# Packed adjacency bytes turned by a DMA transpose of column pairs in a two-layer graph kernel

## The chip, the cores and the metric

The kernel runs on one core of a Trainium2 chip. The time is the device time of one execution in microseconds (us). A core has TensorE (PE; its weight loads are shown apart as PEld), VectorE (DVE), ScalarE (ACT), GpSimd (POOL) and SyncE (SP); 16 DMA engines move data, asked for by SP, ACT or POOL.

## The reference

x is 8192 x 128 in float32, adj is a symmetric 8192 x 8192 int32 matrix of zeros and ones with ones on the diagonal. Two layers follow one another:

```python
o1 = matmul((adj == 1), matmul(V, w1))        # adj == 2 and adj == 3 likewise with w2, w3: empty here
x = layernorm(x + o1 + o2 + o3 + bias)

h = x @ W.T + b
e = (h @ we1 + be1) + (h @ we2 + be2).T
e = where(e >= 0, e, 0.01 * e)
attention = softmax(where(adj > 0, e, -9e15), axis=1)
x = layernorm(x + attention @ h)
```

exp(leaky(e1 + e2)) splits into a product of a row factor and a column factor on either side of e1 + e2 = 0. So the second layer is, like the first, a product of 0/1 masks with tables: one mask of the edges with a positive sum, one of the others.

## The kernel before

The adjacency is read once, in 64 chunks of 1024 rows x 1024 columns: 8 row blocks S, and in each 8 column chunks c (k = 8 S + c). POOL loads a chunk in two halves into one of up to five buffers (L518; the DMA casts int32 to one byte), and asks for the load that reuses a buffer when the chunk that lay there is packed. DVE (`check_and_pack`, L571) packs eight rows of bytes into the eight bits of one byte, in a 128 x 1024 byte tile `pk` (L588). This tile has the rows of the matrix in the partitions, and the products need the columns there. So ACT converts it to bf16 with the byte order changed from (q j) to (j q) (`convert`, L999), TensorE transposes its eight 128x128 pieces into one PSUM bank (`turn`, L1192), and ACT writes the bank as bytes into the store of all edges, `E_raw` (`edges_of`, L1005). DVE then spreads the bits into fp8 masks (`spread`, L591): for layer 0 by `edge_masks` (L601) into `U0`, for layer 1 by `masks` (L606) into `UP`.

Layer 0 of a chunk is 32 TensorE products with 512 columns each (`layer0`, L1177; two halves of 16). After the eight chunks of a row block, its tail (y, the product with w1, layer norm, the score columns, the tables) runs over DVE, ACT, PE and SP; `tails(k)` gives its step by the slot. Layer 1 is 128 batches (`batch`, L1218), each one row half-block by one column chunk, and each 32 products: for every j of 8, two masks (positive in `UP`, negative in `gate_bufs`), and two tables. ACT makes a batch's gates with eight Sign activations of 128x512 into `gate_bufs` (`gates`, L1013); DVE ANDs them with the edges (L614) and XORs the rest (L616).

Each engine runs its own program in a fixed order over slots k = 0, 1, ... (loops at L823 for DVE, L1103 for ACT, L1277 for PE); semaphores alone tie them together. In slot k:

- DVE: `masks` of the slot's batches, `check_and_pack(k)`, `edge_masks(k-1, ...)`, pieces of the tails.
- ACT: `edges_of(k-1)`, gates of the batches of slot k+1, `convert(k)`, pieces of the tails.
- PE: `layer0(k-2, 0)`, `layer0(k-2, 1)`, the slot's batches, `turn(k)`, pieces of the tails.

48 of the 128 batches lie in slots up to 68, beside the chunks (`EARLY`); 80 follow when the whole adjacency has been read. At the end every finished half-block gets its product with W, its quotients, layer norm and a store.

Of the kernel before, what the change touches and what calls it, by code (L numbers as in the profile page):

```python
# [25 lines left out]
ACT = mybir.ActivationFunctionType  # L26
# [111 lines left out]
def build(nc, x, adj, w1, w2, w3, bias, W, b, we1, be1, we2, be2, out):  # L138
# [4 lines left out]
    with ExitStack() as ctx:  # L143
        def sb(name, shape, dt):
            return ctx.enter_context(nc.sbuf_tensor(name, shape, dt))
# [12 lines left out]
        tab_raw = sb("tables", [P, NS * 4 * JC * D], F16)  # L158
        in_raw = sb("adj_in", [P, 4 * 4 * CC], U8)
        seen = sb("seen", [P, 2 * CC], U16)  # L160
        pk = sb("packed", [P, CC], U8)
        pkb = sb("packed_bf16", [P, CC], BF16)
        U0 = sb("edge_masks", [P, 2 * JC * GR], U8)
        UP = sb("pos_masks", [P, 2 * JC * GR], U8)
        GN = sb("neg_masks", [P, 2 * JC * GR], U8)
# [72 lines left out]
        psT = ps[:, 2, :].bitcast(BF16)  # L238

        o_bank = ps[:, 3, :].rearrange("p (t c) -> p t c", t=GT)  # L240

        def o_of_bank(S, h):

            return ps[:, 2, :].rearrange("p (t c) -> p t c", t=GT) if h and S == NS - 1 else o_bank

        def z_bank(q, k):
            return ps[:, 4 + 2 * (q % 2) + k, :]
# [18 lines left out]
        def half(k, h):  # L266
            return homes[HOME[k]][:, 4096 * h:4096 * (h + 1)]

        def bits_of(S, c):
            n = (S * JB + c * JC) * P  # L270
            return E_raw[:, n:n + CC]


        def sems(*names):
# [7 lines left out]
        s_seen, s_p1, s_p2, s_pk, s_conv, s_turn, s_evac, s_u0, s_l0 = sems(  # L282
            "seen", "packed_4", "packed_2", "packed_1", "packed_converted", "packed_turned", "edges_ready",
            "edge_masks_ready", "layer0_multiplied")
# [274 lines left out]
        def _(e):  # L559
# [11 lines left out]
            def check_and_pack(k):  # L571
                e.wait_ge(s_adj[HOME[k]], 32 * FILL[k])
                a8, b8 = half(k, 0), half(k, 1)
                a, bb = a8.bitcast(U32), b8.bitcast(U32)
                w = CC // 4
                e.scalar_tensor_tensor(a, bb, 4, a, ALU.logical_shift_right, ALU.bitwise_or).then_inc(s_p1, 1)  # L576
                e.wait_ge(s_p1, k + 1)
                e.wait_ge(s_seen, k + 1)
                e.tensor_tensor(seen[:, :], seen[:, :], a8.bitcast(U16), ALU.bitwise_or).then_inc(s_seen, 1)  # L579
                e.wait_ge(s_seen, k + 2)  # L580
                low2 = a8[:, 0:2 * CC].bitcast(U16)
                e.tensor_scalar(low2, low2, 0x1111, None, ALU.bitwise_and).then_inc(s_half, 1)
                e.wait_ge(s_half, k + 1)
                e.scalar_tensor_tensor(a[:, 0:2 * w], a[:, 2 * w:], 0x22222222, a[:, 0:2 * w],
                                       ALU.bitwise_and, ALU.bitwise_or).then_inc(s_p2, 1)
                e.wait_ge(s_p2, k + 1)
                ge(e, s_conv, k)
                e.scalar_tensor_tensor(pk[:, :].bitcast(U32), a[:, w:2 * w], 2, a[:, 0:w],  # L588
                                       ALU.logical_shift_left, ALU.bitwise_or).then_inc(s_pk, 1)

            def spread(dst, src, h):  # L591

                src = src.bitcast(U16).rearrange("p (j i) -> p j i", j=JC)
                dst = dst.bitcast(U16).rearrange("p (j n i) -> p j n i", j=JC, n=GT)
                for n in range(GT):
                    by = 4 - BIT[4 * h + n]
                    shift = ALU.logical_shift_left if by >= 0 else ALU.logical_shift_right
                    ins = e.tensor_scalar(dst[:, :, n, :], src, abs(by), MASK, shift, ALU.bitwise_and)  # L598
                return ins

            def edge_masks(k, h):  # L601
                e.wait_ge(s_evac, k + 1)
                ge(e, s_l0, 2 * (k - 1) + h + 1)
                spread(U0[:, 4096 * h:4096 * (h + 1)], bits_of(k // NCH, k % NCH), h).then_inc(s_u0, 1)

# [382 lines left out]
        def _(e):  # L988
# [7 lines left out]
                e.wait_ge(s_vr, v + 1)  # L996
                e.activation(v_hl[:, 1, sl, :], x_in[:, sl, :], ACT.Copy, scale=LOW).then_inc(s_vl, 1)

            def convert(k):  # L999
                e.wait_ge(s_pk, k + 1)  # L1000
                ge(e, s_turn, k)
                e.activation(pkb[:, :].rearrange("p (j q) -> p j q", j=JC),  # L1002
                             pk[:, :].rearrange("p (q j) -> p j q", j=JC), ACT.Copy).then_inc(s_conv, 1)

            def edges_of(k):  # L1005
                e.wait_ge(s_turn, k + 1)
                if k >= 4 * NCH:
                    e.wait_ge(s_vl, NCH)
                if k >= (NS - 1) * NCH:
                    e.wait_ge(s_pk, GUEST[4] + 1)  # L1010
                e.activation(bits_of(k // NCH, k % NCH), psT, ACT.Copy).then_inc(s_evac, 1)  # L1011

            def gates(m):  # L1013
                q, g, c, _, _ = BATCH[m]
                if HELD[m] is not None:
                    e.wait_ge(s_bat, HELD[m] + 1)
                if GATE[m] == 2:
                    e.wait_ge(s_er, NS)
                e.wait_ge(s_row[q % 2], 16 * (q // 2 + 1))
                e.wait_ge(s_er, max(c, g // 2) + 1)  # L1020
                for j in range(JC):
                    n = GR * j
                    ins = e.activation(gate_bufs[GATE[m]][:, n:n + GR].bitcast(I8), e1row[:, q % 2, :], ACT.Sign,  # L1023
                                       bias=t2[:, JC * c + j:JC * c + j + 1])
                ins.then_inc(s_gate, 1)

# [76 lines left out]
            for k in range(NSLOT):  # L1103
                for S, off in tails(k):
                    if off == 3:
                        x1_of(S)
                if 1 <= k <= K:
                    edges_of(k - 1)
                if 1 <= k <= NCH:
                    split_low(k - 1)  # L1110
                for S, off in tails(k):
                    if off == 4:
                        e1_turned(S)
                        b_d_of(S)
                for m in at(k + 1):
                    if not fresh(m):
                        gates(m)
                for S, off in tails(k):
                    if off == 2:
                        sd_of(S)  # L1120
                    if off == 4 and not S:
                        high(S)
                if k < K:
                    convert(k)
# [51 lines left out]
        def _(e):  # L1176
            def layer0(k, h):  # L1177
# [4 lines left out]
                    e.wait_ge(s_y, 2 * (S - 1) + h + 1)  # L1182
                e.wait_ge(s_u0, 2 * k + h + 1)
                for j in range(JC):
                    n = 4096 * h + GR * j
                    for i, kind in enumerate((F8A, F8B)):
                        ins = e.matmul(ps[:, h, :], v_hl[:, i, JC * c + j, :], U0[:, n:n + GR].bitcast(kind),  # L1187
                                       start=c == 0 and j == 0 and i == 0,
                                       stop=c == NCH - 1 and j == JC - 1 and i == 1)
                ins.then_inc(s_l0, 1)  # L1190

            def turn(k):  # L1192
                e.wait_ge(s_conv, k + 1)
                ge(e, s_evac, k)
                for j in range(JC):
                    ins = e.transpose(psT[:, j * P:(j + 1) * P], pkb[:, j * P:(j + 1) * P], idb[:, :])  # L1196
                ins.then_inc(s_turn, 1)

            def o_of(S, h):
                e.wait_ge(s_y, 2 * S + h + 1)  # L1200
                if h:
                    if S < NS - 1:
                        e.wait_ge(s_v, 2 * S + 1)
                elif S:
                    e.wait_ge(s_e1Tc, S)
                else:
                    e.wait_ge(s_setc, 1)
# [10 lines left out]
            def batch(m):  # L1218
# [9 lines left out]
                e.wait_ge(s_pos, m + 1)  # L1228
                both = UP[:, 4096 * (m % 2):4096 * (m % 2 + 1)], gate_bufs[GATE[m]]
                for j in range(JC):  # L1230
                    n = GR * j
# [45 lines left out]
            for k in range(NSLOT):  # L1277
# [11 lines left out]
                if k < K:  # L1289
                    turn(k)  # L1290
                for m in at(k):
                    if first_of_all(m):
                        batch(m)
# [107 lines left out]
```

## Time and profile before

| | us |
|---|---|
| median of 3 runs | 1555.93 (1555.51 to 1557.21) |
| the profiled execution | 1557.76 |
| its span, from first to last instruction | 1556.1 |

| engine | busy us | share of the span |
|---|---|---|
| PE (products) | 1418.2 | 91% |
| PEld (weight loads, beside the products) | 669.7 | 43% |
| DVE | 1106.7 | 71% |
| ACT | 981.2 | 63% |
| POOL | 102.2 | 7% |

The profile page gives for each engine the time in which it was busy, then groups of instructions with their count, mean duration, and the idle time of the engine before them with what ended it. A row such as `PE ps L1196 <- ACT packed_bf L1002` says that TensorE sat idle before instructions of line 1196 until ACT had finished line 1002. The shares are means over the whole span; the kernel has three parts (a first one up to about 160 us, the rest of the chunks up to about 900 us, the batches alone after that), so the views below are also read stretch by stretch. The adjacency loads are in the page's queue 0 (software), everything that SP issues in queue 1 (hardware).

### The profile page before, as it was taken

Reading aid. Unit: us, or ns where it says so; the run is one execution under the profiler, and the core shown is the slowest. Engines: PE = TensorE matmul, PEld = TensorE weight load, DVE = VectorE, ACT = ScalarE, POOL = GpSimd, SP = SyncE. Lnnn points to the kernel's source line nnn. Section 1 sums busy time; section 2 is a strip of 40 time slices with the busy share of each in tenths; the row PEclk is TensorE's granted clock in tenths of the full one; section 3 lists DMA queues with packets and bytes.
Section 4 is the critical chain, followed back from the end, with each engine's and each line's share of the span. In section 5 each row is a group of like instructions: output and inputs, shape, how many; then the busy total and the mean of one; then the engine's idle time right before and its main releaser. Section 6 shows DMA issues by size and latency. Waiting matters only on the chain. (4 is left out here: it accounts for less than half of the span.)

```text
span 1556.1 us, 19556 instructions
## 1 busy us (share of the span) xinstructions
PE 1418.2 (91%) x6934; PEld 669.7 (43%) x6934; DVE 1106.7 (71%) x2561; ACT 981.2 (63%) x1584; POOL 102.2 (7%) x137
## 2 busy tenths in 40 slices
PE   0887798979999999999999997999999999999996
PEld 0434343444444444444444443444444444444443
DVE  2667777877977967967967946577667676666663
ACT  1334527446457457457457558678888788788873
POOL 2111111100110110100101000000000000000000
PEclk9989899999999999999999998999999999999998
DMA  9999999994979779886889421000110000100100
GB/s 125 145 126 116 130 107 140 115 108 76 83 100 115 83 74 102 114 83 75 113 85 102 82 95 55 8 1 28 48 34 28 28 28 27 55 27 28 35 1 15
DMA packets 88980, 114.32 MB, mean 73 GB/s; under 512 B 5104, under 2 KB 71216, under 8 KB 88880
## 3 DMA queue, kind: packets, MB, share of 16 engines
q0 software_dynamic: 67584, 67.12, 47.1%
q1 hardware_dynamic: 21296, 45.92, 8.6%
q8 instruction: 57, 0.93, 0.2%
q14 instruction: 43, 0.35, 0.1%
HBM read 298.06 MB, written 16.29 MB: 202 GB/s over the span
## 5 line engine op out<-in xcount | busy, mean ns | idle before, releaser
L1234 PE MATMUL ps<-pos_masks,tables 128*128 128x512 fp8e4 x2048 | 613.6, 381 | 39.6 <-DVE pos_masks L616 39.6
L1023 ACT ACTIVATE neg_masks<-e_row,cols 128x512 int8<-128x512 f32 x816 | 509.8, 709 | 109.0 <-PE ps L1234 58.4
L1234 PE MATMUL ps<-neg_masks,tables 128*128 128x512 fp8e4 x1632 | 489.7, 382 | 0.0
L1187 PE MATMUL ps<-edge_masks,tables 128*128 128x512 fp8e4 (+1 forms) x2048 | 463.9, 385 | 0.0
L1234 PEld LDWEIGHTS ps<-pos_masks,tables 128*128 128x128 f16 x2048 | 199.6, 98 | 285.8 <-issue 57.0
L1187 PEld LDWEIGHTS ps<-edge_masks,tables 128*128 128x128 f16 x2048 | 201.6, 99 | 233.2 <-issue 13.3
L1234 PEld LDWEIGHTS ps<-neg_masks,tables 128*128 128x128 f16 x1632 | 160.6, 98 | 195.8 <-issue 5.5
L614 DVE TENSOR_TENSOR neg_masks<-pos_masks,neg_masks 128x2048 uint16<-128x2048 uint16 x102 | 125.0, 1225 | 92.6 <-ACT neg_masks L1023 89.9
L598 DVE TENSOR_SCALAR pos_masks<-edges 128x512 uint16<-128x512 uint16 x512 | 114.4, 286 | 89.4 <-PE ps L1234 89.4
L1002 ACT ACTIVATE packed_bf<-packed 128x1024 bf16<-128x1024 uint8 x64 | 72.3, 1130 | 149.4 <-DVE packed L588 149.4
L598 DVE TENSOR_SCALAR edge_masks<-edges 128x512 uint16<-128x512 uint16 x512 | 124.2, 308 | 54.4 <-PE ps L1187 53.4
L1011 ACT ACTIVATE edges<-ps 128x1024 uint8<-128x1024 bf16 x64 | 65.1, 1017 | 148.1 <-PE ps L1196 147.8
L1023 ACT ACTIVATE y_turned<-e_row,cols 128x512 int8<-128x512 f32 x208 | 130.0, 707 | 22.5 <-DMA e_row<-e_scratch 12.1
L616 DVE TENSOR_TENSOR pos_masks<-pos_masks,neg_masks 128x2048 uint16<-128x2048 uint16 x102 | 124.9, 1225 | 3.5
L1234 PE MATMUL ps<-y_turned,tables 128*128 128x512 fp8e4 x416 | 123.7, 379 | 0.0
L1196 PE MATMUL ps<-idb,packed_bf 128*128 128x128 bf16 x512 | 42.5, 231 | 81.9 <-ACT packed_bf L1002 81.7
L518 POOL DMA_DIRECT2D adj_in<-adj x84 | 66.3, 793 | 536.4 <-DVE packed L588 525.0
L703 DVE TENSOR_TENSOR a_c_rows<-ps,a_c_rows 128x512 f32<-128x512 f32 x68 | 43.7, 684 | 52.1 <-PE ps L1234 48.9
L1196 PEld LDWEIGHTS ps<-idb,packed_bf 128*128 128x128 bf16 x512 | 35.0, 103 | 101.1 <-ACT packed_bf L1002 60.8
L576 DVE SCALAR_TENSOR_TENSOR adj_in<-adj_in 128x1024 uint32<-128x1024 uint32 x42 | 51.2, 1219 | 36.9 <-DMA adj_in<-adj 36.9
L1234 PEld LDWEIGHTS ps<-y_turned,tables 128*128 128x128 f16 x416 | 40.7, 98 | 49.1
L579 DVE TENSOR_TENSOR seen<-seen,adj_in 128x2048 uint16<-128x2048 uint16 x42 | 51.4, 1225 | 1.4
(134 smaller groups left out, 850.5 us busy)
## 6 DMA issues: line engine op xcount, KB each, us to landing
adj_in<-adj POOLq DMA_DIRECT2D x84, 512.0 KB, 13.7
tables<-adj POOLq DMA_DIRECT2D x28, 512.0 KB, 32.3
e_row<-e_scratch SPq DMA_DIRECT2D x34, 256.0 KB, 3.9
edges<-adj POOLq DMA_DIRECT2D x16, 512.0 KB, 12.5
part_scratch<-a_c_rows SPq DMA_DIRECT2D x18, 256.0 KB, 4.1
part_in<-part_scratch SPq DMA_DIRECT2D x18, 256.0 KB, 3.1
edges<-x SPq DMA_DIRECT2D x8, 512.0 KB, 6.6
x_rows<-x SPq DMA_DIRECT2D x8, 512.0 KB, 7.2
```

Source lines behind the costliest of these rows:

```text
L518: e.dma_start(half(k, h).bitcast(F8C).rearrange("p (b c) -> p b c", b=GT), block_rows(adj, S)[:, GT * h:GT * (h + 1), c * CC:(c + 1) * CC])\
L576: e.scalar_tensor_tensor(a, bb, 4, a, ALU.logical_shift_right, ALU.bitwise_or).then_inc(s_p1, 1)
L579: e.tensor_tensor(seen[:, :], seen[:, :], a8.bitcast(U16), ALU.bitwise_or).then_inc(s_seen, 1)
L598: ins = e.tensor_scalar(dst[:, :, n, :], src, abs(by), MASK, shift, ALU.bitwise_and)
L614: e.tensor_tensor(n, u, n, ALU.bitwise_and).then_inc(s_neg, 1)
L616: e.tensor_tensor(u, u, n, ALU.bitwise_xor).then_inc(s_pos, 1)
L1002: e.activation(pkb[:, :].rearrange("p (j q) -> p j q", j=JC), pk[:, :].rearrange("p (q j) -> p j q", j=JC), ACT.Copy).then_inc(s_conv, 1)
L1011: e.activation(bits_of(k // NCH, k % NCH), psT, ACT.Copy).then_inc(s_evac, 1)
L1023: ins = e.activation(gate_bufs[GATE[m]][:, n:n + GR].bitcast(I8), e1row[:, q % 2, :], ACT.Sign, bias=t2[:, JC * c + j:JC * c + j + 1])
L1187: ins = e.matmul(ps[:, h, :], v_hl[:, i, JC * c + j, :], U0[:, n:n + GR].bitcast(kind), start=c == 0 and j == 0 and i == 0, stop=c == NCH ...
L1196: ins = e.transpose(psT[:, j * P:(j + 1) * P], pkb[:, j * P:(j + 1) * P], idb[:, :])
L1234: ins = e.matmul(z_bank(q, k), tab[:, c, 2 * k + i, j, :], mask[:, n:n + GR].bitcast(F8A), start=first and j == 0 and i == 0, stop=final a ...
```

## The change

The eight TensorE transposes of a chunk, the conversion in front of them and the PSUM evacuation behind them go. In their place ACT issues one DMA transpose for each chunk, in the slot and at the place where it converted. It works on 2-byte elements, so a pair of neighbouring bytes moves together; therefore the last packing step writes `pk` in a new order, with the pair index outermost, through 16-bit instead of 32-bit words; it reads its two sources with a step of 8 bytes. In the partition of one column pair the bytes of columns 2j' and 2j'+1 now alternate. The masks and the gates keep that order: `place(mask, j)` names the 512 bytes of one j, which lie every second byte, and both the ACT instruction that writes a gate and the TensorE products that read a mask use it. `pk` has two buffers, each with a semaphore of its own; the packing waits for the transpose of two chunks ago. Products of the first layer's second half with w1 get a PSUM bank of their own in all row blocks (bank 2, free now), and with it one wait goes.

```diff
-        pk = sb("packed", [P, CC], U8)
-        pkb = sb("packed_bf16", [P, CC], BF16)
+        pk = sb("packed", [P, 2, CC], U8)
...
         def o_of_bank(S, h):
-            return ps[:, 2, :].rearrange("p (t c) -> p t c", t=GT) if h and S == NS - 1 else o_bank
+            return ps[:, 3 - h, :].rearrange("p (t c) -> p t c", t=GT)
...
+        def place(mask, j):
+            return mask[:, 2 * GR * (j // 2):2 * GR * (j // 2 + 1)].rearrange("p (i two) -> p two i", two=2)[:, j % 2, :]
...
             # check_and_pack, DVE
-                ge(e, s_conv, k)
-                e.scalar_tensor_tensor(pk[:, :].bitcast(U32), a[:, w:2 * w], 2, a[:, 0:w],
+                if k >= 2:
+                    e.wait_ge(s_edges[k % 2], 16 * (k // 2))
+                w1, w0 = [a8[:, CC * n:CC * (n + 1)].bitcast(U16).rearrange("p (q j) -> p j q", j=JC // 2)
+                          for n in (1, 0)]
+                e.scalar_tensor_tensor(pk[:, k % 2, :].bitcast(U16).rearrange("p (j q) -> p j q", j=JC // 2), w1, 2, w0,
                                        ALU.logical_shift_left, ALU.bitwise_or).then_inc(s_pk, 1)
...
             # spread, DVE
-                src = src.bitcast(U16).rearrange("p (j i) -> p j i", j=JC)
-                dst = dst.bitcast(U16).rearrange("p (j n i) -> p j n i", j=JC, n=GT)
+                src = src.bitcast(U16).rearrange("p (j i) -> p j i", j=JC // 2)
+                dst = dst.bitcast(U16).rearrange("p (j n i) -> p j n i", j=JC // 2, n=GT)
...
             # edge_masks, DVE
-                e.wait_ge(s_evac, k + 1)
+                e.wait_ge(s_edges[k % 2], 16 * (k // 2 + 1))
...
             # ACT, in slot k where convert(k) stood; edges_of(k - 1) at the slot's start is gone
-            def convert(k):
+            def turn(k):
                 e.wait_ge(s_pk, k + 1)
-                ge(e, s_turn, k)
-                e.activation(pkb[:, :].rearrange("p (j q) -> p j q", j=JC),
-                             pk[:, :].rearrange("p (q j) -> p j q", j=JC), ACT.Copy).then_inc(s_conv, 1)
...
-                e.activation(bits_of(k // NCH, k % NCH), psT, ACT.Copy).then_inc(s_evac, 1)
+                e.dma_start_transpose(bits_of(k // NCH, k % NCH).bitcast(U16).rearrange("p (j q) -> p j q", j=JC // 2),
+                                      pk[:, k % 2, :].bitcast(U16)).then_inc(s_edges[k % 2], 16)
...
             # gates, ACT
-                    ins = e.activation(gate_bufs[GATE[m]][:, n:n + GR].bitcast(I8), e1row[:, q % 2, :], ACT.Sign,
+                    ins = e.activation(place(gate_bufs[GATE[m]], j).bitcast(I8), e1row[:, q % 2, :], ACT.Sign,
...
             # layer0, PE
-                        ins = e.matmul(ps[:, h, :], v_hl[:, i, JC * c + j, :], U0[:, n:n + GR].bitcast(kind),
+                        ins = e.matmul(ps[:, h, :], v_hl[:, i, JC * c + j, :],
+                                       place(U0[:, 4096 * h:4096 * (h + 1)], j).bitcast(kind),
...
             # PE
-            def turn(k):
-                e.wait_ge(s_conv, k + 1)
-                ge(e, s_evac, k)
-                for j in range(JC):
-                    ins = e.transpose(psT[:, j * P:(j + 1) * P], pkb[:, j * P:(j + 1) * P], idb[:, :])
-                ins.then_inc(s_turn, 1)
...
             # o_of, PE
-                if h:
-                    if S < NS - 1:
-                        e.wait_ge(s_v, 2 * S + 1)
-                elif S:
+                if S:
                     e.wait_ge(s_e1Tc, S)
...
             # batch, PE
-                            ins = e.matmul(z_bank(q, k), tab[:, c, 2 * k + i, j, :], mask[:, n:n + GR].bitcast(F8A),
+                            ins = e.matmul(z_bank(q, k), tab[:, c, 2 * k + i, j, :], place(mask, j).bitcast(F8A),
```

## Rows read from the trace of the kernel before

**Rows 1.** Busy time by stretch: start:end, length, then each engine's busy us (instructions), clock, DMA.

```profile
core 0: us, PE busy (x) PEld busy (x) DVE busy (x) ACT busy (x) POOL busy (x), PEclk, DMA share, GB/s
0.00:160.00 160.00, 99.11 (x473) 48.57 (x474) 96.06 (x210) 54.32 (x72) 27.74 (x42) 0.93 1.09 127
160.00:280.00 120.00, 102.39 (x517) 48.31 (x514) 92.43 (x223) 60.65 (x100) 14.20 (x19) 0.94 1.12 125
280.00:400.00 120.00, 106.54 (x529) 50.79 (x529) 94.40 (x211) 62.10 (x102) 10.97 (x14) 0.96 0.81 97
...
637.00:754.00 117.00, 116.10 (x594) 55.55 (x593) 93.38 (x211) 69.90 (x117) 11.00 (x14) 1.00 0.77 91
...
1000.00:1250.00 250.00, 249.19 (x1182) 116.81 (x1181) 171.92 (x414) 204.13 (x325) 0.51 (x1) 1.00 0.08 26
```

**Rows 2.** Waits in 0 to 160 us: waiting line, releaser, total us, times, longest us.

```profile
PE ps L1196 <- ACT packed_bf L1002: 58.7, 9, 29.7
...
DVE adj_in L576 <- DMA adj_in<-adj: 34.7, 6, 20.6
...
DVE tables L576 <- DMA tables<-adj: 15.7, 6, 5.1
```

**Rows 3.** Timeline of DVE, first stage, the last packing step of four chunks (start, duration).

```profile
61.50 0.42 DVE L588 SCALAR_TENSOR_TENSOR packed<-tables 128x256 uint32<-128x256 uint32 x1
...
72.73 0.42 DVE L588 SCALAR_TENSOR_TENSOR packed<-adj_in 128x256 uint32<-128x256 uint32 x1
```

**Rows 4.** The same, after the last piece of x has been loaded.

```profile
126.24 0.42 DVE L588 SCALAR_TENSOR_TENSOR packed<-adj_in 128x256 uint32<-128x256 uint32 x1
...
136.14 0.42 DVE L588 SCALAR_TENSOR_TENSOR packed<-tables 128x256 uint32<-128x256 uint32 x1
```

**Rows 5.** Waits over the whole span.

```profile
PE ps L1196 <- ACT packed_bf L1002: 81.7, 17, 29.7
...
DVE edge_masks L598 <- ACT edges L1011: 0.8, 1, 0.8
```

**Rows 6.** Waits of TensorE and DVE in 520 to 900 us.

```profile
PE ps L1234 <- DVE pos_masks L616: 4.6, 4, 1.9
...
DVE adj_in L576 <- DMA adj_in<-adj: 2.2, 1, 2.2
```

**Rows 7.** Timeline at 748 us: the transposes' weight loads, then layer 0's, on TensorE.

```profile
748.39 0.65 PEld L1196 LDWEIGHTS ps<-idb,packed_bf 128*128 128x128 bf16 x8
...
749.00 6.63 PEld L1187 LDWEIGHTS ps<-edge_masks,tables 128*128 128x128 f16 x32
```

**Rows 8.** Chain that ended last: start, us, what; 256 products in a row.

```profile
1445.05 55.25 PE ps L1234 x256
```

**Rows 9.** Groups by line and form: busy us, mean ns of one, idle before.

```profile
L1023 ACT ACTIVATE neg_masks<-e_row,cols 128x512 int8<-128x512 f32 x816 | 509.8, 709 | 109.0 <-PE ps L1234 58.4 <-issue 39.8 <-DMA e_row<-e_scratch 10.8
...
L1002 ACT ACTIVATE packed_bf<-packed 128x1024 bf16<-128x1024 uint8 x64 | 72.3, 1130 | 149.4 <-DVE packed L588 149.4
...
L1011 ACT ACTIVATE edges<-ps 128x1024 uint8<-128x1024 bf16 x64 | 65.1, 1017 | 148.1 <-PE ps L1196 147.8
...
L584 DVE SCALAR_TENSOR_TENSOR adj_in<-adj_in 128x512 uint32<-128x512 uint32 x42 | 29.1, 693 | 1.4
...
L588 DVE SCALAR_TENSOR_TENSOR packed<-adj_in 128x256 uint32<-128x256 uint32 x42 | 17.8, 424 | 1.4
```

**Rows 10.** Timeline at 760 us on DVE: a chunk packed, and its masks begun.

```profile
760.48 0.42 DVE L588 SCALAR_TENSOR_TENSOR packed<-adj_in 128x256 uint32<-128x256 uint32 x1
...
770.18 0.89 DVE L598 TENSOR_SCALAR edge_masks<-edges 128x512 uint16<-128x512 uint16 x4
```

**Rows 11.** DMA issues: KB each, median us from issue to landing.

```profile
part_in<-part_scratch SPq DMA_DIRECT2D x18, 256.0 KB, 3.1
...
x_rows<-x SPq DMA_DIRECT2D x8, 512.0 KB, 7.2
```

**Rows 12.** DMA queue of SP: packets, MB, share of 16 engines over the span.

```profile
q1 hardware_dynamic: 21296, 45.92, 8.6%
```

More of the change, by code:

```diff
@@ L237, in build @@
         ps = ctx.enter_context(nc.psum_tensor("ps", [P, 8, GR], F32))
-        psT = ps[:, 2, :].bitcast(BF16)
-        o_bank = ps[:, 3, :].rearrange("p (t c) -> p t c", t=GT)
         def o_of_bank(S, h):
-            return ps[:, 2, :].rearrange("p (t c) -> p t c", t=GT) if h and S == NS - 1 else o_bank
+            return ps[:, 3 - h, :].rearrange("p (t c) -> p t c", t=GT)
         def z_bank(q, k):
@@ L281, in build @@
         s_adj = [sem(f"adj_in_{n}") for n in range(5)]
-        s_seen, s_p1, s_p2, s_pk, s_conv, s_turn, s_evac, s_u0, s_l0 = sems(
-            "seen", "packed_4", "packed_2", "packed_1", "packed_converted", "packed_turned", "edges_ready",
-            "edge_masks_ready", "layer0_multiplied")
+        s_seen, s_p1, s_p2, s_pk, s_u0, s_l0 = sems(
+            "seen", "packed_4", "packed_2", "packed_1", "edge_masks_ready", "layer0_multiplied")
+        s_edges = [sem(f"edges_ready_{n}") for n in range(2)]
         s_y, s_xg, s_xb, s_o, s_v, s_st, s_mv, s_var, s_sd, s_rs, s_nm, s_x1 = sems(
@@ L997, in split_low @@
                 e.activation(v_hl[:, 1, sl, :], x_in[:, sl, :], ACT.Copy, scale=LOW).then_inc(s_vl, 1)
-            def convert(k):
+            def turn(k):
                 e.wait_ge(s_pk, k + 1)
-                ge(e, s_turn, k)
-                e.activation(pkb[:, :].rearrange("p (j q) -> p j q", j=JC),
-                             pk[:, :].rearrange("p (q j) -> p j q", j=JC), ACT.Copy).then_inc(s_conv, 1)
-            def edges_of(k):
-                e.wait_ge(s_turn, k + 1)
                 if k >= 4 * NCH:
                     e.wait_ge(s_vl, NCH)
-                if k >= (NS - 1) * NCH:
-                    e.wait_ge(s_pk, GUEST[4] + 1)
-                e.activation(bits_of(k // NCH, k % NCH), psT, ACT.Copy).then_inc(s_evac, 1)
+                e.dma_start_transpose(bits_of(k // NCH, k % NCH).bitcast(U16).rearrange("p (j q) -> p j q", j=JC // 2),
+                                      pk[:, k % 2, :].bitcast(U16)).then_inc(s_edges[k % 2], 16)
             def gates(m):
@@ L1021, in gates @@
                 for j in range(JC):
-                    n = GR * j
-                    ins = e.activation(gate_bufs[GATE[m]][:, n:n + GR].bitcast(I8), e1row[:, q % 2, :], ACT.Sign,
+                    ins = e.activation(place(gate_bufs[GATE[m]], j).bitcast(I8), e1row[:, q % 2, :], ACT.Sign,
                                        bias=t2[:, JC * c + j:JC * c + j + 1])
@@ L1106, in _ @@
                         x1_of(S)
-                if 1 <= k <= K:
-                    edges_of(k - 1)
                 if 1 <= k <= NCH:
@@ L1123, in _ @@
                 if k < K:
-                    convert(k)
+                    turn(k)
                 if k < NCH:
@@ L1184, in layer0 @@
                 for j in range(JC):
-                    n = 4096 * h + GR * j
                     for i, kind in enumerate((F8A, F8B)):
-                        ins = e.matmul(ps[:, h, :], v_hl[:, i, JC * c + j, :], U0[:, n:n + GR].bitcast(kind),
+                        ins = e.matmul(ps[:, h, :], v_hl[:, i, JC * c + j, :],
+                                       place(U0[:, 4096 * h:4096 * (h + 1)], j).bitcast(kind),
                                        start=c == 0 and j == 0 and i == 0,
@@ L1230, in batch @@
                 for j in range(JC):
-                    n = GR * j
                     for k, mask in enumerate(both):
                         for i in range(2):
-                            ins = e.matmul(z_bank(q, k), tab[:, c, 2 * k + i, j, :], mask[:, n:n + GR].bitcast(F8A),
+                            ins = e.matmul(z_bank(q, k), tab[:, c, 2 * k + i, j, :], place(mask, j).bitcast(F8A),
                                            start=first and j == 0 and i == 0, stop=final and j == JC - 1 and i == 1)
@@ L1288, in _ @@
                         after(m)
-                if k < K:
-                    turn(k)
                 for m in at(k):
```

## The prediction

> **What bounds the kernel now.** I read the busy time by stretch first, since the shares over the whole span mix three parts [rows 1]. From 1000 us on TensorE is busy 249.19 of 250 us: batches alone, and no chunk is turned there. From 637 to 754 us, which is eight chunks (14.63 us each), it is busy 116.10 of 117 us; DVE has 93.38 and ACT 69.90. So between about 400 and 900 us TensorE sets the pace, and what it no longer has to do is time won. The waits agree: from 520 to 900 us the batches waited for DVE for only 4.6 us, and DVE for a load of adjacency for 2.2 us [rows 6]. The first 160 us are different. TensorE is busy 99.11 of 160 us, the DMA share is 1.09 [rows 1], and DVE waited 34.7 + 15.7 us for adjacency, 20.6 of it for the first chunk [rows 2]. Chunks are packed every 11.23 us (61.50 to 72.73) while a 512 KB piece of x comes with each, and every 9.90 us (126.24 to 136.14) afterwards [rows 3, 4]. This is the pace of the loads: some 12 chunks are DMA-bound. From 160 to 400 us, some 17 chunks, TensorE is busy 87% (102.39 + 106.54 of 240), the loads still fill the DMA engines in the first half (1.12) but DVE hardly waits for them, and TensorE loses the rest to waits and to stretches at the lower clock (mean granted 0.94 and 0.96) [rows 1].
>
> **TensorE loses the transposes.** The weight loads of eight transposes begin at 748.39 and those of the next products at 749.00, so turning a chunk holds TensorE for 0.61 us [rows 7]. (The durations of single matmuls overlap; I count starts.) In the 12 DMA-bound chunks that is worth nothing, since TensorE idles there anyway. In the other 52 it is 52 x 0.61 = 31.7 us. That holds for the 35 chunks from 400 us on without doubt, and for the 17 before them as far as TensorE is on the path; it is at 87%, so I count them too.
>
> **TensorE loses a wait.** It waited 81.7 us for the converted bytes [rows 5], 58.7 of them in the first 160 us, where 29.7 is the start [rows 2]. Behind 160 us there are 81.7 - 58.7 = 23.0 us. In their place TensorE goes on to layer 0 two chunks back, whose masks come from DVE; next late are DVE's masks and the tails. So of the 23 us I take a third, 8 us, with 0 and 20 as ends. The bank for the second w1 product takes a wait on DVE away at seven places; it was short of the path, and I count nothing.
>
> **ACT.** It loses a conversion of 1130 ns and an evacuation of 1017 ns for each chunk [rows 9], 2.15 us, and the waits for TensorE in front of the evacuation. It gets the issue of a DMA. Its hold on ACT's queue is in no row; gates, high parts of tables and exponentials are queued behind it. ACT idles 117 - 69.90 = 47 us in eight chunks, 5.9 us each [rows 1], so with the 2.15 us freed a hold of up to 8 us a chunk fits on average. Cost 0 for the likely case; above 8 us ACT would be the bound.
>
> **The gates and the strided masks.** ACT now writes every second byte. The nearest rows are the two operations of 1024 elements: with bytes read at a step of 8 it took 1130 ns, with dense ones 1017 [rows 9]. Scaled to 512 elements that is 57 ns on 709, at most 0.46 us for the eight gates of a batch. In the last part ACT is busy 204.13 of 250 us [rows 1], so it goes to 87% and stays hidden by TensorE except at the ends of half-blocks; I take 0, with up to +8 us. The 6144 products of 512 columns read fp8 at a step of 2 bytes. They start 55.25 / 256 = 0.216 us apart [rows 8], one column per tick of the 2.4 GHz clock, which a dense row of bytes doesn't show to be free at a step of two. I take 0 and keep the other case as a rival.
>
> **DVE.** The last packing step goes from 256 words (424 ns) to 512 half-words; the row with 512 elements took 693 ns [rows 9]. That is +0.27 us a chunk, 17 us in all, with DVE at 80% in the steady part [rows 1]: hidden. A step of 8 bytes may add to it; even a doubling is hidden. The masks are spread with as many elements as before. The new wait in front of the packing is on a transpose of two chunks ago, which is old by then.
>
> **Latency of the transpose.** `edge_masks` waits for it. Queued behind that wait on DVE are the masks of the next batches and the next packing. A chunk packed at 760.90 has its masks begun at 770.18, and it is among the tightest [rows 10]; in the DMA-bound part it is about 9.5 us as well. Today DVE waits 0.8 us for the evacuation in all [rows 5]. Transfers of SP landed in 3.1 us (256 KB) and, beside the loads, 7.2 us (512 KB) [rows 11]. A chunk is 128 KB, so 3 to 7 us are hidden. Beyond 9 us DVE would stall, and TensorE behind it.
>
> **DMA work of the transpose.** This is the cost that matters, because it adds to each chunk in the DMA-bound part: x us more of the 16 engines give 12 x. Lower bound: 512 KB of x stretched a chunk by 11.23 - 9.90 = 1.33 us, so 128 KB cost 0.33 us [rows 3, 4]. Upper bound: SP's queue shows 21296 packets in 8.6% of 16 x 1556.1 us, 0.10 us a packet [rows 12]; if a chunk is cut into 512 pieces of 256 bytes it costs 512 x 0.10 / 16 = 3.2 us. I take 1.0 us, between them in ratio: +12 us, ends +4 and +38. From 160 us on it is covered: the loads need 9.90 us of the 14.63 us of a chunk.
>
> The two rules of the Trainium skill that bear on this contradict each other. "DMA: Bandwidth & Descriptors", in its list of oddities, gives the DMA transpose 261 GB/s; by an estimate from it 128 KB take 0.5 us, the term would be +6 us and the forecast 1526. "VectorE: DVE Perf Modes", section on the three transpose paths, puts a 128x128 transpose at 1309 ns by DMA and 390 ns on TensorE, and advises TensorE where PSUM will do as the destination, which speaks against this change. On the TensorE side the trace disagrees if it is meant as a rate: eight took 0.61 us, 76 ns each [rows 7]. If its DMA figure were work of the engines, an estimate gives four blocks 5.2 us a chunk, the rival B below.
>
> **Clock.** In the first 160 us the mean granted clock is 0.93 with TensorE 62% busy [rows 1]. It will do slightly less and idle in one piece instead of two. Half a dozen more short stretches at 1.2 GHz could cost a few us where TensorE is just late: +4, between 0 and +12.
>
> **Sum.** -31.7 - 8 + 12 + 4 = -24 us on the span of 1556.1. The profiled execution (1557.76) lies 1.8 us above the median of 1555.93; on the median it gives 1532. With the ends of the terms: -31.7 - 20 + 4 = -48, 1508; -21 (if the 17 middle chunks give nothing) - 0 + 38 + 12 + 8 = +37, 1593.
>
> **Rival A: more than the sum.** The coupling of ACT and TensorE in both directions goes, and the middle part gets the whole of its waits back: 1495 to 1510. For it: ACT waited for TensorE in front of L1011 for 147.8 us [rows 9]. Against: most of that is idle time which ACT has anyway. Chance 0.13.
>
> **Rival B, the slower side: the DMA engines.** The transposes compete with the adjacency loads. In the first 12 chunks each us counts; beyond 14.63 - 0.61 - 9.90 = 4.1 us all other 52 chunks become DMA-bound too. The change is lost from x = 3.0 on (12 x 3 = 36 = 31.7 + 8 - 4). At x = 4.5: 54 + 52 x 0.4 = 75, less 36, is +39: 1595. At x = 5.2: 62 + 57 - 36 = +83: 1639. For it: a DMA share of 1.09 and 1.12 up to 280 us [rows 1], and a transpose may move small pieces. Against: 128 KB are little beside the 1 MB of bytes that a chunk's load writes. A hold of over 8 us on ACT would look much the same in time. Chance 0.26.
>
> **Rival C: strided operands.** If TensorE reads bytes at a step of two at half rate, 6144 x 0.216 = 1327 us are added: 2860. A loss of 2% would already eat the gain. Nothing in the trace speaks for it but that no row shows the step. Chance 0.05.
>
> **Rival D: nothing.** The gain in the middle part and the loss in the first cancel (x near 3, or half the gain): 1553 to 1559. Chance 0.06. The forecast, 1510 to 1553, has 0.50.
>
> **How the numbers follow.** 0.2%, 3 us, is about what a measurement of this kernel can tell from no change. Faster: 0.50 + 0.13 = 0.63; same 0.06; slower 0.26 + 0.05 = 0.31. The range leaves out C, the part of B beyond 1600 (some 0.08), and half of A: 1500 to 1600.
>
> **What the profile will show.** The 0.61 us: eight chunks in the steady part take 117.0 - 4.9 = 112 us. The first part: the spacing of packings is 9.90 + x. ACT: no wait before the place where it converted, and gates near 709 ns. Latency: DVE's wait before `edge_masks` stays near nothing. Strides: TensorE's products still start 0.216 us apart, and the packing step takes some 0.69 us. I am wrong if the spacing in the first part is over 13 us, if DVE waits for the transposes, or if ACT's activations stand apart by many us after each issue.

## The result, and the profile after

| | before | changed |
|---|---|---|
| median of 4 runs, us | 1556.33 (1555.51 to 1557.21) | 1600.79 (1600.12 to 1601.61) |
| span of the profiled execution, us | 1556.1 | 1599.7 |

The ratio is 1.0287, with a 95% interval of 1.0275 to 1.0299: 44 us slower. The forecast was 1532 us, faster, with a range up to 1600.

The busy time by stretch, in the columns of [rows 1]:

```profile
core 0: us, PE busy (x) PEld busy (x) DVE busy (x) ACT busy (x) POOL busy (x), PEclk, DMA share, GB/s
0.00:160.00 160.00, 84.95 (x346) 36.38 (x346) 88.55 (x188) 23.95 (x29) 26.37 (x40) 0.91 1.10 130
160.00:280.00 120.00, 91.15 (x400) 40.56 (x401) 87.33 (x202) 34.60 (x79) 13.70 (x18) 0.87 1.12 126
...
637.00:754.00 117.00, 110.96 (x513) 50.47 (x510) 91.27 (x199) 52.50 (x96) 11.03 (x14) 0.99 0.84 100
...
1000.00:1250.00 250.00, 242.00 (x1138) 112.87 (x1137) 169.22 (x391) 203.36 (x325) 0.51 (x1) 0.99 0.10 29
```

TensorE lost work and did not become faster for it: in the steady part it is busy 110.96 of 117 us where it was 116.10. ACT lost what it should, 52.50 us against 69.90. The last chunk is packed at 931.0 us against 886.5, so the whole loss of 44 us has come by then, 30.1 us of it by chunk 40 (575.5 against 545.4); the part with batches alone takes as long as before (668.7 against 669.6 us from there to the end).

Who waited in 520 to 900 us, from the waits of the changed kernel (to be read against [rows 6]):

```profile
ACT neg_masks L1016 <- PE ps L1214: 107.7, 15, 15.5
...
PE ps L1214 <- DVE pos_masks L617: 14.8, 5, 4.0
...
DVE edge_masks L599 <- DMA edges<-packed: 10.1, 3, 3.5
...
PE ps L1197 <- DVE cols L663: 5.0, 3, 1.8
```

DVE waits for the transpose, 3.4 us in each of three row blocks, and TensorE for DVE. The chain of waits of 690 to 800 us shows how one hangs on the other (start, length, what):

```profile
737.40 11.93 DMA edges<-packed
749.57 0.69 DVE edge_masks L599 x3
750.26 1.13 DVE y_turned L655
751.39 1.14 DVE x_rows L655
...
763.46 1.21 ACTq L1004
764.79 1.92 ACT y_turned L1065 x7
...
769.78 3.07 ACT neg_masks L1016 x6
...
774.75 1.24 DVE neg_masks L615
...
785.47 1.64 DVE y_turned L683 x7
...
789.83 1.80 DVE h_part L671
...
794.04 1.24 DVE pos_masks L617
795.42 4.85 PE ps L1214 x11
```

The transpose takes 11.93 us from its issue to its landing. Behind it come the edge masks, the sums for e1 and e2, the next packing, on ACT the high parts of the tables and gates, on DVE low parts and row sums and the masks of a batch, and only then TensorE.

What the transposes cost themselves: the queues' rows on the profile's page, the view of line 1004 over the whole span, and the same view in 905 to 940 us, at the end of the loads:

```profile
q0 software_dynamic: 67584, 67.12, 46.4%
...
q10 hardware_dynamic: 34816, 8.40, 3.7%
```

```profile
L1004 ACTq DMA_TRANSPOSE edges<-packed x64: 1205/1207/1433, 25.3 to 931.7; - x64
...
DMA to landing us min/median/max: 2.4/10.1/12.5
```

```profile
DMA to landing us min/median/max: 2.4/4.5/5.2
```

A transpose holds ACT for 1.21 us and takes 0.037 x 1599.7 / 64 = 0.92 us of all 16 engines. It lands after 10.1 us in the median. The three of the last view are issued at 906.3, 922.4 and 931.7 us and land after 4.5, 5.2 and 2.4 us; the last loads are issued by 906.6 us, and the mean busy share of the DMA engines is 0.72 in 920 to 930 us and 0.06 in 930 to 940. So only the 2.4 us are those of a transpose with the engines nearly to itself.

### The profile page after: what moved, and what is told of

Its sections match the earlier page's. It is cut to its first block, busy times and chain, and to the rows that moved or that the text cites. A ratio compares the mean times of both kernels' runs of the same rounds, so it can differ in the third digit from the quotient of the medians.

```text
span 1599.7 us, 18341 instructions
## 1 busy us (share of the span) xinstructions
PE 1403.2 (88%) x6422; PEld 639.8 (40%) x6422; DVE 1125.6 (70%) x2561; ACT 855.3 (53%) x1456; POOL 101.8 (6%) x137
## 3 DMA queue, kind: packets, MB, share of 16 engines
q0 software_dynamic: 67584, 67.12, 46.4%
q1 hardware_dynamic: 21296, 45.92, 8.6%
## 4 chain that ended last, share of the span: by engine, by line
PE 42%; DVE 13%; ACT 8%; DMA 3%; issue 3%; ACTq 0%; SPq 0%; DVEq 0%
PE ps L1214 35%; PE ps L1177 6%; ACT neg_masks L1016 4%; DMA edges<-packed 3%; DVE neg_masks L615 2%; DVE edge_masks L599 1%; ACT y_turned L1016 1%; DVE a_c_rows L704 1%; DVE pos_masks L617 1%; DVE pos_masks L599 1%; PE ps L1228 1%; DVE seen L577 1%; DVE h_part L671 1%; ACT tables L1065 1%; DVE adj_in L574 1%
## 5 line engine op out<-in xcount | busy, mean ns | idle before, releaser
L1177 PE MATMUL ps<-edge_masks,tables 128*128 128x512 fp8e4 (+1 forms) x2048 | 471.5, 390 | 67.1 <-DVE edge_masks L599 67.0
L1070 ACT ACTIVATE a_c_rows<-a_c_rows 128x1024 f32<-128x1024 f32 x34 | 35.7, 1051 | 38.8 <-DVE a_c_rows L697 38.6
L615 DVE TENSOR_TENSOR y_turned<-pos_masks,y_turned 128x2048 uint16<-128x2048 uint16 x26 | 31.9, 1225 | 19.7 <-ACT y_turned L1016 19.0
L1027 ACT ACTIVATE y_turned<-ps 128x512 f32<-128x512 f32 x16 | 8.7, 588 | 68.1 <-PE ps L1177 68.1
```

Of the source, the lines that this page charges most:

```text
L615: e.tensor_tensor(n, u, n, ALU.bitwise_and).then_inc(s_neg, 1)
L1070: e.activation(ac[:, :, :], ac[:, :, :], ACT.Exp).then_inc(s_exp, 1)
L1177: ins = e.matmul(ps[:, h, :], v_hl[:, i, JC * c + j, :], place(U0[:, 4096 * h:4096 * (h + 1)], j).bitcast(kind), start=c == 0 and j == 0 a ...
```

## The experiments

Two figures of the traces stand beside the times here: when chunk 40 is packed, and how long eight steady chunks take (start of the last packing step of chunk 54 less that of chunk 46). They are figures of one traced execution each, the medians of four to ten executions.

| kernel | median us | ratio to before, 95% | chunk 40 at, us | eight chunks, us |
|---|---|---|---|---|
| before | 1556.33 | | 545.4 | 117.08 |
| changed | 1600.79 | 1.0287 (1.0275 to 1.0299) | 575.5 | 121.65 |
| pairs_on_pe | 1556.90 | 0.9999 (0.9990 to 1.0009) | 545.3 | 117.12 |
| no_transpose | 1558.82 | 1.0021 (1.0009 to 1.0034) | 546.2 | 116.21 |
| plain_dma_copy | 1559.50 | 1.0021 (1.0012 to 1.0031) | 550.8 | 118.70 |
| plain_copy_256 | 1587.97 | 1.0206 (1.0184 to 1.0229) | 568.0 | 120.63 |
| sums_first | 1580.04 | 1.0153 (1.0136 to 1.0170) | 561.7 | 118.28 |
| transpose_two_moves | 1575.39 | 1.0119 (1.0100 to 1.0138) | 563.4 | 116.60 |
| transpose_all_moves | 1543.40 | 0.9921 (0.9900 to 0.9941) | 555.3 | 112.43 |
| no_transpose_tables_later | 1528.70 | 0.9822 (0.9800 to 0.9843) | 541.7 | 112.40 |
| before_tables_later | 1545.46 | 0.9932 (0.9911 to 0.9952) | 543.1 | 116.03 |
| before_all_moves | 1543.31 | 0.9904 (0.9882 to 0.9925) | 541.2 | 116.14 |
| first16_on_pe | 1535.66 | 0.9861 (0.9844 to 0.9878) | 551.5 | 112.47 |
| first40_on_pe | 1536.67 | 0.9878 (0.9861 to 0.9894) | 545.1 | 112.43 |

### Is it the layout? pairs_on_pe

The kernel before, with masks, gates and edges in pairs; the evacuation writes every second byte:

```diff
-                e.activation(bits_of(k // NCH, k % NCH), psT, ACT.Copy).then_inc(s_evac, 1)
+                e.activation(bits_of(k // NCH, k % NCH).rearrange("p (j q two) -> p j two q", j=JC // 2, two=2),
+                             psT.rearrange("p (j two q) -> p j two q", j=JC // 2, two=2), ACT.Copy).then_inc(s_evac, 1)
```

> The old way (conversion, eight TensorE transposes, evacuation), with masks, gates and edges in the new paired order; the evacuation writes every second byte. Theory L (the transpose lands too late beside the adjacency loads; the layout costs nothing): 1555 to 1560 us, matmuls still 0.216 us apart, gates 710 ns. Rival S (bytes at a step of two cost TensorE or ACT something that the new trace spreads over many waits): above 1570 us, towards 1600.

It took 1556.90 us, the time of the kernel before. The gates in its trace, which now write at a step of two bytes:

```profile
L1027 ACT ACTIVATE neg_masks<-e_row,cols 128x512 int8<-128x512 f32 x816 | 510.1, 711 | 106.4 <-PE ps L1236 58.5 <-issue 38.2 <-DMA e_row<-e_scratch 9.7
```

711 ns against 709 [rows 9], and the matmuls' mean durations did not change either. The layout costs nothing, and rival C is out.

### Without the transpose: no_transpose

```diff
-                e.dma_start_transpose(bits_of(...).bitcast(U16).rearrange("p (j q) -> p j q", j=JC // 2),
-                                      pk[:, k % 2, :].bitcast(U16)).then_inc(s_edges[k % 2], 16)
+                e.activation(bits_of(k // NCH, k % NCH), pk[:, k % 2, :], ACT.Copy).then_inc(s_edges[k % 2], 1)
```

> The changed kernel with the DMA transpose left out: ACT copies the 1024 bytes of a chunk instead, about 1 us of ACT, so the bits stay unturned and the result is not the reference's. Packing, strides, order and PSUM banks are those of the changed kernel. Theory L: the loss and more goes, about 1520 to 1530 us, eight chunks of the steady part take some 112 to 113 us and the first part is back at 9.90 us a chunk. Rival D (the 0.27 us more of packing, or the order without the transposes on TensorE, is what costs): it stays over 1570 us.

1558.82 us. That removes the loss, but there is no gain at all, where 1520 to 1530 was expected: TensorE has 512 transposes fewer, and the kernel is no faster. Its packing takes 341.2 us from chunk 40 to chunk 63, where the kernel before took 341.1. (The counts that DVE waits for change with the edit; they aren't shown.) Its timeline at 756 us, with TensorE's wait:

```profile
755.32 1.22 DVE L617 TENSOR_TENSOR pos_masks<-pos_masks,neg_masks 128x2048 uint16<-128x2048 uint16 x1
...
756.69 0.59 PE L1213 MATMUL ps<-pos_masks,tables 128*128 128x512 fp8e4 x2 [3.66 <-DVE pos_masks L617]
...
758.84 1.06 PE L1213 MATMUL ps<-pos_masks,tables 128*128 128x512 fp8e4 x2
```

In the kernel before the same instruction of DVE began at 755.64, and TensorE started this batch at 757.01 after a wait of 0.89 us. DVE is as early or late as ever, and TensorE waits 3.66 us. Then, from 757.98 to 761.40 us, two matmuls take 1.06 us where they take 0.59: the granted clock of this stretch is 0.50, the lower of TensorE's two levels, and about half of the 3.4 us is lost. In the kernel before it stays at 1.00 behind the wait of 0.89 us. So two things bound the steady part before, not one: TensorE's work, and a chain through DVE and ACT which returns once in each row block.

### Pieces or turning? plain_dma_copy and plain_copy_256

The same 128 KB, copied and not turned. In the first kernel `dma_start` takes the place of `dma_start_transpose`. In the second the packed tile has gaps of 256 bytes, so that the copy is cut in as many pieces as the transpose:

```diff
-        pk = sb("packed", [P, 2, CC], U8)
+        pk = sb("packed", [P, 2, 4, 2, CC // 4], U8)
...
+                e.dma_start(bits_of(k // NCH, k % NCH).rearrange("p (j q) -> p j q", j=4),
+                            pk[:, k % 2, :, 0, :]).then_inc(s_edges[k % 2], 16)
```

> The changed kernel with an ordinary DMA copy of the same 128 KB in place of the transpose, issued by ACT at the same place; the bits stay unturned, so the result is not the reference's. Theory L in the form that the many 256-byte pieces wait one by one behind load packets (34 packets an engine, about 0.17 us each): with 8 pieces of 1 KB an engine it lands within 4 to 6 us and the time is 1525 to 1540 us. Rival Q (any DMA issued by ACT waits in line behind the loads, whatever its pieces): it lands after 8 us or more and the time stays near 1590 to 1600 us.

> The plain DMA copy again, but cut in 512 pieces of 256 bytes like the transpose (the packed tile has gaps, so pieces can't merge); bits unturned, result not the reference's. Theory P (pieces: each one of an engine's 32 waits behind a load packet): it lands at about 10 us as the transpose does, chunks of the first part cost what they cost with the transpose, and the time is 1590 to 1601 us. Rival X (the turning itself is what takes the time): it lands near 6 us like the copy in pieces of 1 KB, 1558 to 1565 us.

Queue 10, the copy's row in the DMA view, and the landing in the view of its line; first in the trace of plain_dma_copy:

```profile
q10 hardware_dynamic: 9216, 8.39, 1.8%
...
edges<-packed ACTq DMA_DIRECT2D x64, 128.0 KB, 6.0
```

and in that of plain_copy_256:

```profile
q10 hardware_dynamic: 33792, 8.39, 3.2%
...
edges<-packed ACTq DMA_DIRECT2D x64, 128.0 KB, 10.1
```

The copy in pieces of 1 KB lands after 6.0 us, as expected, and takes 1559.50 us, which by the medians is hardly more than no DMA at all. By the traces it is not quite free: chunk 40 is packed 4.6 us later than in no_transpose, whose traced execution was its fastest, 1555.98 us. The expected 1525 to 1540 us was missed because it counted on TensorE's gain, which no_transpose doesn't have either. Cut in 256-byte pieces the same bytes land after 10.1 us, just as the transpose does, and the time is 1587.97, 2 us under the expected range. Each engine gets 9216 / 64 / 16 = 9 packets a chunk in one and 33 in the other; (10.1 - 6.0) / 24 = 0.17 us for each more. A load's packet takes 0.464 x 16 x 1599.7 / 67584 = 0.176 us. So what the pieces wait for is most simply this: each waits for one packet of the load in front of it. Two landing times give this slope but don't test it. The page "DMA: Bandwidth & Descriptors" of the Trainium skill, section "Queues, rings and completion order", describes such turns: each engine goes round the queues it has work for, one packet at a time, with typically some 9 to 17 descriptors in a packet. The traces agree with turns; whether a packet in the profile's count is one in the sense of that page, and so how many pieces go in one turn, no run here shows.

Turning itself is not what makes it late. The 13 us between 1587.97 and 1600.79 remain to it: the transpose holds ACT for 1.21 us, the copy for 0.60, and it uses 0.92 us of the engines against 0.032 x 1585.9 / 64 = 0.79. I have no run that splits these 13 us further.

### Covering the wait: sums_first and transpose_two_moves

On DVE, in the third slot of a tail:

```diff
+                for S, off in tails(k):
+                    if off == 3:
+                        e_sums(S)
                 if 1 <= k <= K:
                     edge_masks(k - 1, 0)
                 for S, off in tails(k):
                     if off == 2:
                         statistics(S)
-                    if off == 3:
-                        e_sums(S)
```

> The changed kernel with one move on DVE: in the third slot of a tail the sums for e1 and e2 (4.9 us of work) come before the edge masks that wait for the transpose. Theory L: the 3.3 us wait before these masks at 749 us is covered, the turning of e1 on TensorE comes earlier, and each eight chunks of the steady part lose some 4 us less: 1580 to 1588 us. Rival D or S: no change, 1598 to 1603 us.

1580.04 us, 20.8 us less for a move of 4.9 us of work. In the second kernel, ACT also issues the transpose ahead of the square root that waits for the variances; `turn(k)` goes in front of `sd_of(S)`. In the changed kernel the issue at 737.40 stands right behind that square root.

> The changed kernel with the sums ahead of the edge masks and the transpose issued ahead of the square root, but tables and row sums where they were. Theory L and C: DVE no longer waits for the transpose in the steady part, but the tail's chain still binds as it does without any transpose, so eight steady chunks take about 117 us and the time is 1565 to 1572 us. If latency were all, it would already be near the 1543 us of all moves.

It took 1575.39 us, 4.6 less again but 3 more than the bound of the expectation; the first part keeps more of its loss than I had thought. The steady part does what was expected: 116.60 us for eight chunks, which is what it takes without any transpose (116.21). There DVE has no wait for a transpose left in 520 to 900 us, but TensorE still waits 17.5 us for DVE's masks, as it waits 15.0 us without any transpose. The latency is repaired in this part, and the second loss is left.

### The other bound: no_transpose_tables_later, before_tables_later and transpose_all_moves

On DVE, the row sums, and from the third row block on the low parts of the table, go behind the masks of the next batch:

```diff
-                    if off == 4 + min(S, 1):
+                    if off == 4 + min(S, 2):
                         low(S)
-                    if off == 5:
+                    if off == 6:
                         rows_sum(S)
```

> The kernel without the transpose, in which DVE makes the low parts of a table and the row sums (6.6 us) one slot later, behind the masks of the next batch. Theory C (the DVE and ACT chain of a tail binds each row block together with TensorE, so the 4.9 us that TensorE saves in eight chunks turn into its wait at 757 us plus a stretch at the lower clock): the wait goes, eight chunks take 112 to 113.5 us, and the time is 1530 to 1545 us. Rival (the period is held by something else, such as the loads or ACT): it stays at 1555 to 1560 us.

> The kernel before with the same move of low parts and row sums to one slot later. Theory C: it has only the wait of about 1 us in each row block to win, so 1549 to 1556 us. If the move by itself were worth more (1535 to 1545 us), the run without the transpose would prove nothing about the saving on TensorE.

> The changed kernel with three moves: the sums for e1 and e2 ahead of the edge masks (DVE), the issue of the transpose ahead of the square root that waits for the variances (ACT), and the low parts and row sums one slot later (DVE). Theory L and C together: the transpose lands in time from 400 us on and TensorE's saving appears; 1555 to 1568 us, with some 8 to 10 us lost in the first 12 chunks to the DMA engines. If latency were not the cause of the loss, it would stay at the 1580 us of the first move alone.

The same two lines give the kernel before 11 us, by the ratios 0.7%, and the kernel without the transpose 30 us (1558.82 to 1528.70, 1.3 us under its expected range). Only when the chain is out of the way does it show that TensorE does less. Like must be compared with like: before_tables_later takes 116.03 us for eight chunks and no_transpose_tables_later 112.40, and TensorE is busy 100% of 520 to 900 us in both. So the transposes are worth 3.6 us in eight chunks, 0.45 us each, and not the 0.61 that had been worked out. (The 117.08 us before hold a wait of about 1 us besides.) In all, leaving them out gives 16.8 us (1545.46 to 1528.70), and by chunk 40 only 1.4 of these have come (543.1 against 541.7). before_tables_later gave more than the 0 to 7 us expected; I had counted its steady wait alone and not the loss in the middle part. The kernel with the real transpose and all three moves is at 1543.40, 57 us faster than the change as it was made. That is 12 us under the expected 1555 to 1568: behind the first two moves (1575.39) the third alone gives 32 us, as much as the kernel without a transpose gets from it. TensorE has no wait left in its steady part. Its busy time in 637 to 754 us:

```profile
637.00:754.00 117.00, 117.00 (x552) 54.05 (x551) 100.57 (x216) 56.85 (x104) 11.09 (x14) 1.00 0.95 104
```

But before_all_moves shows that this is no win for the transpose:

> The kernel before with the same three moves. With TensorE turning the chunks it stays TensorE's pace: eight steady chunks 116.0 us as with the one move, and 1543 to 1547 us in all. So the moves by themselves would not be worth more than 10 us to it, and what all moves give to the kernel with the transpose (57 us) would be the repair of its own two losses. If it came to 1535 us or less, the DMA transpose would have nothing left in its favour.

The kernel before, with TensorE turning the chunks and the same three moves (its conversion takes the place of the transpose's issue), takes 1543.31 us. The transpose wins 3.7 us in each eight steady chunks and has lost 14.1 us by chunk 40 (555.3 against 541.2).

### Only where it pays: first16_on_pe and first40_on_pe

`ON_PE` chunks are turned on TensorE as before, into the paired order, the rest by DMA; all three moves. Shown is ACT's program, where the issue stands; the transposes and evacuations come back with it:

```diff
-                if k < K:
+                if k < ON_PE:
+                    convert(k)
+                elif k < K:
                     turn(k)
```

> The transposed kernel with all three moves, in which the first 16 chunks are turned on TensorE as before (conversion, eight transposes, evacuation into the paired order) and the other 48 by DMA. Theory W (while the loads bind, a transpose's DMA work adds 0.7 to 0.8 us to each chunk, and its late landing costs some more there, whereas TensorE idles): 8 us less than the 1543 us of all moves, 1533 to 1537 us, the chunks of the first part at 9.90 us again and eight steady chunks still 112.4 us. Rival: if the first part's loss has another cause (packing, strides), it stays at 1541 to 1545 us.

> As the kernel that turns the first 16 chunks on TensorE, but the first 40. Up to there (555 us in the trace of all moves) TensorE has idle time anyway, and with the DMA transpose the chunks 16 to 40 took 340 us against 330 us in the kernel before with the same moves. Theory W and L (the DMA transpose is only worth something where TensorE is full): these 10 us come back, and the last 24 chunks keep 3.7 us for each eight; 1524 to 1531 us. Rival (the 10 us belong to something else in the changed kernel): 1533 to 1538 us.

With 16 chunks on TensorE the chunks of the first part are back at 9.90 us (packed at 104.94, 114.84, 124.75), and the time is 1535.66 us, as expected. It beats both kernels: 1.4% less than before. With 40 chunks the expectation of 1524 to 1531 was missed: 1536.67. The trace packs chunk 40 at 545.1 us and not at 551.5, so 6 of the 10 us seem to have come back; of these the eight chunks from 40 to 48 lose 1.6 (114.05 against 112.47 us). But the traced execution is the fastest of its four (1535.99 us) and that of first16_on_pe the slowest (1539.57), and the medians of the two kernels can't be told apart. How the rest goes is open.

## Why the prediction was wrong

**TensorE loses the transposes: the step that failed.** What failed is "what it no longer has to do is time won", counted for 52 chunks. I read 116.10 of 117 us busy as the bound, and the waits of [rows 6] as none: 4.6 us in four waits. But four waits in 380 us is one in each row block, and here it was the end of another chain, as long as TensorE's own work. Without the transposes, chunks 40 to 63 took 341.2 us as before (341.1), and the full 31.7 us came to nothing (no_transpose, 1558.82). The size was off too. [rows 7] takes the 0.61 us from the starts of weight loads. These run ahead of their products, the transposes' by 0.22 us and layer 0's by 0.05. The starts of the products themselves, in the kernel before:

```profile
748.61 0.61 PE L1196 MATMUL ps<-idb,packed_bf 128*128 128x128 bf16 x8
749.05 7.07 PE L1187 MATMUL ps<-edge_masks,tables 128*128 128x512 fp8e4 x32
```

That is 0.44 us, and the kernels without waits say 0.45. For 52 chunks it would be 23 us. Of these the 17 chunks in the middle gave next to nothing even with the chain out of the way, 1.4 us by chunk 40; TensorE's other waits there are for DVE and ACT.

**TensorE loses a wait.** 8 us were taken for it, and none of it showed: without any transpose chunk 40 is packed at 546.2 us, against 545.4 before. The masks of DVE were named as the next late thing, and they were; the price of that was left out of the large term.

**Latency: the second step that failed.** "3 to 7 us are hidden" was bounded by transfers of SP, which go in packets of 2.2 KB on average (45.92 MB in 21296 [rows 12]). The transpose goes in 34 packets an engine, and landed after 10.1 us (2.4 to 12.5). The cover, the time from packing to masks that hides it, was read as 9 us where it is shortest [rows 10]. In the third slot of a tail the cover starts later, since ACT issues the transpose only after the square root, 4 us behind the packing; there 11.93 us were too much. DVE waited for transposes nine times, 30.6 us in all, which the prediction had named as a sign of being wrong. Cutting the same bytes in 256-byte pieces costs 28.5 us (1587.97 against 1559.50). Most of that is latency; a part is engine time, 0.79 us a chunk against 0.018 x 1558.6 / 64 = 0.44.

**DMA work: near, and partly by luck.** 1.0 us a chunk was taken; it is 0.92 by the queue's share. In the first part chunks 6 to 9 were packed at 100.20 and 131.80, 10.53 us each, against 9.90 in [rows 4]: 0.6 us, not 1.0. At chunk 11 the changed kernel was 7.1 us late and at chunk 12 12.0 us, where 12 had been taken. The last 4.9 us are another thing, a wait for the transpose in the tail of the first row block:

```profile
153.14 0.69 DVE L589 SCALAR_TENSOR_TENSOR packed<-tables 128x512 uint16<-128x512 uint16 x1
159.84 0.90 DVE L599 TENSOR_SCALAR edge_masks<-edges 128x512 uint16<-128x512 uint16 x4 [6.01 <-DMA edges<-packed]
...
169.89 0.69 DVE L589 SCALAR_TENSOR_TENSOR packed<-adj_in 128x512 uint16<-128x512 uint16 x1
```

**Rival B** had the right sign and place, the transposes beside the loads, but a wrong mechanism: no work of the engines of 3 us or more, but time in line. The Trainium skill's figure of 1309 ns for a 128x128 transpose ("VectorE: DVE Perf Modes", "The three transpose paths") is no rate here: four blocks cost 0.92 us of the engines and landed after 2.4 us at best. The Trainium skill's rate of 261 GB/s in "DMA: Bandwidth & Descriptors", "Latency and other measured facts" (0.5 us, as an estimate from it) is nearer.

**ACT, strides, packing: right.** ACT is held for 1.21 us and was never the bound. Gates 710 ns, packing step 692 ns against the 693 expected, products as fast as before.

**Clock.** +4 us was probably sized too small. By the mean clocks of the stretches up to 1000 us, TensorE lost (1 - 0.91) x 160 + (1 - 0.87) x 120 and so on, 51.7 us, to the lower level; before it was 28.4. Of these 23 us some fall where TensorE had time to spare, so they bound the cost and don't give it. From 400 to 520 us the mean went from 1.00 to 0.94: a TensorE that has to wait comes back slower for a few microseconds.

The sum for the changed kernel, in the order of the runs: 1556.3 before; +2.5 without any transpose, where -31.7 - 8 had been taken; +0.7 for a DMA copy of the bytes; +28.5 for cutting it in 256-byte pieces; +12.8 for turning them. That is 1600.8. (The medians come from several chips, on which the kernel before took 1555.3 to 1556.6 us; the ratios in the table say the same.)

## What to carry to other kernels

An engine that is busy 99% with one short wait in each period need not be the only bound: before counting its saved work as time, find the chain that ends in that wait, and ask how much longer the period could get without it. Take the size of the saving from the starts of the products themselves, not of their weight loads. The latency of a small DMA depended here on its number of pieces and on what its engines were already carrying; read the cover of each place where it is waited for from its issue on, and put independent work there first. Two such moves gave 25 us of the 44 back, and three gave the kernel before 13 us with no DMA transpose at all.

## What was not expected of the hardware

- 128 KB in 512 pieces landed after 10.1 us beside loads, in 128 pieces after 6.0, and a transpose in 2.4 us when the engines had almost nothing else.
- TensorE reads fp8 at a step of two bytes, and ACT writes int8 at that step, at the dense rate (711 ns against 709); DVE combined 512 half-words read at a step of 8 bytes in 692 ns, as long as 512 dense words.
- A wait of 3.66 us on TensorE was followed by 3.4 us at a granted clock of 0.50 (1.06 us for two products instead of 0.59). In that row block the longer wait (3.66 us against 0.89) and the half rate cost about 4.5 us, where eight chunks had saved 3.6.
